# Two V projections of a half visit moved ahead of the scores on TensorE, in the attention of a six-layer network

## What is computed

```python
for i in range(DEPTH):                                  # DEPTH = 6
    x = attn_layer(shift_tokens(x), Wqkv[i], q_scale[i], k_scale[i], Wo[i]) + x
    x = ffn_layer(shift_tokens(x), ln_g[i], ...) + x

def attn_layer(x, Wqkv, qs, ksc, Wo):
    q, k, v = jnp.split(x @ Wqkv, 3, -1)                # 16 heads x 64
    q = l2norm(q) * qs;  k = l2norm(k) * ksc            # then rotary products on q and k
    out = local_attention(q, k, v)                      # windows of 32 queries x 64 keys
    return out.transpose(0, 2, 1, 3).reshape(b, n, INNER) @ Wo
```

## Time and profile before

| | |
|---|---|
| median of 3 runs | 5682.57 us (5681.54 to 5702.88) |
| the profiled execution's own time | 5641.73 us |
| its span in the trace | 5639.9 us |
| TensorE clock granted over the span | 0.916 of full |
| stretch of the six layers | about 1265 to 5600 us |
| busy in the span: PE, PEld, DVE, ACT, POOL | 4558.5, 3064.2, 3371.8, 2396.0, 2573.2 us |

### The profile page before, as it was taken

The page is one execution under the profiler, slowest core; times in us unless marked ns, Lnnn a source line. Parts: engine busy times, 40 slices in busy tenths (PEclk is TensorE's granted clock), DMA queues, the critical chain, the costliest instruction groups (busy, mean ns, idle before and its releaser), DMA issues. The chain is left out here.

```text
span 5639.9 us, 183409 instructions
## 1 busy us (share of the span) xinstructions
PE 4558.5 (81%) x70227; PEld 3064.2 (54%) x70227; DVE 3371.8 (60%) x7024; ACT 2396.0 (42%) x5161; POOL 2573.2 (46%) x4541
## 2 busy tenths in 40 slices
PE   8999838668888878888888888877788887888885
PEld 6777616544555545555555555555555555555553
DVE  3555441666666666665666666666566665666665
ACT  4555443124444344443444444444434444344441
POOL 0000000107666366663566645656546665366661
PEclk9999869879999999999999999989999999999998
DMA  1000003011111010101110111110101011011100
GB/s 34 4 4 3 1 0 98 6 37 28 26 25 29 24 33 22 29 22 30 26 29 22 28 30 26 24 27 22 37 19 29 22 28 37 19 24 27 28 22 31
DMA packets 76047, 143.02 MB, mean 25 GB/s; under 512 B 19655, under 2 KB 57749, under 8 KB 68117
## 3 DMA queue, kind: packets, MB, share of 16 engines
q1 hardware_dynamic: 75284, 131.92, 9.5%
HBM read 35.40 MB, written 4.19 MB: 7 GB/s over the span
## 5 line engine op out<-in xcount | busy, mean ns | idle before, releaser
L2439 DVE TENSOR_TENSOR n_tt<-n_pp,n_rot 128x1024 f32<-128x1024 f32 x768 | 923.4, 1222 | 693.4 <-ACT n_sq L2307 690.5
L1941 POOL TENSOR_TENSOR n_pre<-n_tt 128x512 f32<-128x512 f32 x768 | 969.9, 1274 | 802.8 <-DVE n_tt L2439 802.6
L2057 PE MATMUL n_pp<-n_wqkv,n_xT 128*128 128x512 f32 x1536 | 811.8, 631 | 6.3 <-ACT n_xT L2302 5.6
L2312 ACT COPY n_V<-n_pp 128x512 f32<-128x512 f32 x384 | 224.7, 585 | 1391.1 <-PE n_pp L2065 1391.1
L1976 POOL TENSOR_TENSOR n_pre<-n_pre,n_rn 128x512 f32<-128x512 f32 x768 | 776.6, 1042 | 36.8 <-POOL n_rn L1964 36.8
L2108 PE MATMUL n_pS<-n_qkT 64*32 64x64 f32 (+1 forms) x24576 | 359.4, 233 | 362.9 <-issue 362.9
L2307 ACT ACTIVATE n_sq<-n_pp 128x512 f32<-128x512 f32 x768 | 457.0, 595 | 158.5 <-PE n_pp L2057 152.8
L2108 PEld LDWEIGHTS n_pS<-n_qkT 64*32 64x32 f32 x24576 | 294.5, 110 | 396.2 <-issue 396.2
L2446 DVE TENSOR_REDUCE n_ss<-n_sq 128x8 f32<-128x512 f32 x768 | 504.2, 676 | 0.0
L2065 PE MATMUL n_pp<-n_wqkv,n_xT 128*64 128x512 f32 x1536 | 484.4, 760 | 0.0
L2074 PE MATMUL n_pp<-ident,n_pre 128*128 128x128 f32 x3072 | 420.7, 280 | 72.2 <-POOL n_pre L1976 70.2
(11 more groups left out here) (263 smaller groups left out, 7918.6 us busy)
## 6 DMA issues: line engine op xcount, KB each, us to landing
n_Vx<-n_V SPq DMA_DIRECT2D x192, 256.0 KB, 3.9
n_Vx<-n_V SPq DMA_DIRECT2D x192, 192.0 KB, 3.2
n_wqkv<-in_L_ffn_Wqkv SPq DMA_DIRECT2D x6, 1536.0 KB, 7.4
e_w<-in_L_ffn_w SPq DMA_DIRECT2D x32, 256.0 KB, 3.0
m_Y<-e_ye SPq DMA_DIRECT2D x64, 64.0 KB, 2.0
n_wo<-in_L_ffn_Wo SPq DMA_DIRECT2D x6, 512.0 KB, 7.2
a_xs<-in_L_attn_x SPq DMA_DIRECT2D x16, 128.0 KB, 2.1
x_kept<-X SPq DMA_DIRECT2D x1, 2048.0 KB, 8.6
```

The lines of the kernel that those rows point to most:

```text
L1941: nc.gpsimd.tensor_tensor(d, s[0], s[1][:, :, ::-1, :], ALU.add).then_inc(s_add, 1)
L2057: nc.tensor.matmul(pp[:, c % 2, :], xT[:, j * P:(j + 1) * P], wqkv[:, t * I + 512 * half:t * I + 512 * half + 512], start=True, stop=True) ...
L2439: nc.vector.tensor_tensor(tt[:, c % 4, :, :].rearrange("p s (h d) -> p s h d", d=D), bcast(pp[:, c % 2, :].rearrange("p (h d) -> p h d", d ...
```

## The change

In every half visit that has `nxt`, the two `project_v` calls stand between `weigh` and `scores` instead of behind `scores`. The wait for the turned q and k (`s_qkT`), which stood ahead of the masks, goes with them: it now stands behind `weigh`, ahead of the V projections. In the last visit of a layer all stays as it was. The code of the other engines is the same.

```diff
                     elif prev:
                         weights_ready(pairs[0], N - 1, 1 - u, 1)
-                    after(pe, s_qkT, 8 * N + 4 * j + 4)
+                    if not nxt:
+                        after(pe, s_qkT, 8 * N + 4 * j + 4)
                     masks(N, j)
                     if j == 1:
                         weigh(u, 0)
                     elif prev:
                         weigh(1 - u, 1)
+                    if nxt:
+                        after(pe, s_qkT, 8 * N + 4 * j + 4)
+                        project_v(N + 1, 2 * j, bank("v", 2 * j, 1))
+                        project_v(N + 1, 2 * j + 1, bank("v", 2 * j + 1, 1))
                     scores(j)
                     if nxt:
-                        project_v(N + 1, 2 * j, bank("v", 2 * j, 1))
-                        project_v(N + 1, 2 * j + 1, bank("v", 2 * j + 1, 1))
                         project_qk(N + 1, 4 * j)
                         project_qk(N + 1, 4 * j + 1)
```

## The result

Four runs of the changed kernel have a median of 5491.33 us (5486.06 to 5502.58), against 5688.01 us (5681.54 to 5702.88) for the kernel before on the same chips: ratio 0.9653, 95% interval 0.9626 to 0.9680, 197 us less. The forecast was 5595 us, 87 less than the median that it was taken off; its range, 5480 to 5685, holds the time only just. The direction was right, and nearly every row that was to show a step moved as foretold, but the gain was over twice as large.

What follows compares the result with a forecast made beforehand. It took TensorE's order, with instruction-block stalls in the scores, to bound the kernel. Terms 111 x 0.07 + 39 x 1.55 + 30 x 0.45 + 5 = 87 us, off the median's 5682.6, gave 5595 us; range 5480 to 5685.

Steps and rivals of the forecast that it cites:

- Step 1: Instruction stall in the scores: V ahead of them cuts it from 1.95 to 0.4 us per half visit.
- third rival: The stall stays (chance 0.10): each run of scores pays a fixed stall, wherever V stands; 5866 us.
- the second with its stall of 0.8 us: Rival "even" (chance 0.16): next block comes later, or POOL's last norm holds the turns of q and k; 5668 us.
- Step 2: Behind the scores: V's 1.87 us covered a chain to the second output turn; only 0.42 us come back.
- first rival: All comes through (chance 0.12): no wait opens behind the scores, V's move costs nothing; 343 us less, 5340.
- Step 3: Clock during V projections: of 69 slow half visits, 39 turn fast, gaining 1.55 us each; 30 stay slow, gaining 0.45.
- 39 x 1.55: Term for half visits whose V turns from slow to fast: 39 of them at 1.55 us each, 60 us.
- stays near 92 us: Issue stall ahead of the weighing, 91.6 us in 84 pieces, was to remain unchanged.
- Step 4: Moved wait for turned q and k: worth at most its 5.6 us idle ahead of the masks, taken as 5.
- stall r: Stall left in the scores per half visit: 0.4 us expected, bounds 0 and 1.0, break-even at 0.88.

Runs made afterwards that it cites:

- e5: Changed kernel with the wait back ahead of the masks and the V projections in the middle of the scores: 5620.12 us, ratio 0.9925 to the kernel before.
- e6: Changed kernel with the wait back ahead of the masks and the V projections in the middle of the weighing: 5524.36 us, ratio 0.9762 to the kernel before.
- e4: Changed kernel with add_attention on DVE between the first two rotates instead of behind both: 5304.36 us, ratio 0.9359 to the kernel before.
- e9: Kernel before with add_attention on DVE between the first two rotates, V projections still behind the scores: 5652.44 us, ratio 0.9951.
- e10: e4 with ACT's first square ahead of the first exponential: 5254.44 us, ratio 0.9250 to the kernel before.
- e3: Kernel before with only the wait moved behind the weighing, plus one counter increment, V left behind the scores: 5597.39 us, ratio 0.9877.
- e2: Changed kernel with the wait for turned q and k put back ahead of the masks: 5498.11 us, ratio 0.9715 to the kernel before.
- e1: The kernel before once more, no edit, for a second profiled execution: 5663.93 us, ratio 1.0004.

## Why the prediction was right and wrong

**Step 1, the stall: right.** A block of 256 instructions comes some 3.5 to 4 us after the one before was entered; 0.4 us per half visit were to be left, and 75.7 / 180 = 0.42 are. e5 shows that V has to stand ahead of the stall, and e6 that a place just ahead of the block will do. The third rival, a fixed stall, is out, and the second with its stall of 0.8 us or a new wait for POOL (the turns of q and k wait 56.0 us for its norms, 70.2 before). The Trainium skill, "Runtime: NRT & Kernel Launch", section "Instruction fetch mechanics", calls the cost of a block mostly hidden. In rows of 5.9 ns an instruction it was not: 362.9 us.

**Step 2, what V covered: right.** In the half visit shown, 5.81 us against 5.85, and a wait of 1.61 against 1.65; e4, e9 and e10 show that it is that chain. The first rival is out. For half visits at the full clock the sum of steps 1 and 2, -0.07 us each, came in at -0.09, in part because misses cancel: over the 89, weighing to V takes 0.32 us more, scores 1.72 less (forecast 1.55), and from the end of the scores, V left out, 1.31 more (forecast 1.45).

**Step 3, the clock: the step that failed, by its size.** The mechanism was right, and so was the number of slow half visits left (30 against 29, in the place foretold). The term "39 x 1.55" was too small in both factors. A half visit that turns fast gained 2.61 us, not 1.55. Of the 1.06 us between them, 0.62 are the stall in the weighing, which the forecast held fixed ("stays near 92 us"); 0.20 are a stall in the scores of 2.16 us, where I gave every slow half visit the mean of 1.95; 0.38 are the stretch behind, which already took 4.71 us before in these 56 where I had 4.33 from one of them, so the chain's 5.85 costs less; V gave 0.16 less (1.36 where I had 1.52). Over the 56 that is 59 us. And I had 39 of them, from one mean of 760 ns, where the trace has 56: 17 x 1.55 is 26 us. Together these are the whole way from the 60 us of that term to the measured 146. A mean V is a blunt count: many of before's slow V were only partly at the lower clock.

**Step 4, the moved wait: wrong.** Priced at its own idle time, 5 us; e3 measured 70 us for it alone by the ratio, and with V moved it is 7 to 35 us. It acts on the stall in the weighing: of the fall from 1.57 to 0.62 us in the second half visits of the body, 0.63 us come with the wait (e2 against the changed kernel). So its gain is a part of what step 3 lacked and isn't to be added to it.

**The base.** The sum was taken off an execution 46 us under the median of before, and the median of after lies 4 us over its own profiled execution. 197 - 155 = 42 us of the result are this difference. e1's profile shows more slow V (83 half visits against 77) at the same stalls and is 20 us longer, so about half of it is that the execution that I worked from had fewer slow half visits than usual. Where the rest comes from is open; the medians of before on the other chips were 5660.55, 5667.1 and 5675.08 us, not 5688. Taking the sum off the median as it stood left this out.

That the range holds the time is luck: its lower part was kept for a smaller stall r and for V fast everywhere, and neither came.

## What to carry to other kernels

Where a long run of very short TensorE instructions shows idle time that waits for nothing, count the instructions between two such pauses; if the count is the same each time, put long instructions that are needed anyway within or just ahead of that stretch, and try the semaphore wait ahead of it in another place. Before moving work, ask what it was cover for: here the 1.87 us of V gave back only 0.55 behind the scores (the mean of the 89 half visits at the full clock), until two lines on DVE and one on ACT shortened the chain that it had covered. And price a stall not by its mean but where it stands: two of them in one half visit go with the lower clock.

## What was not expected of the hardware

- A wait that costs next to nothing by its own idle time (5.6 us in all) was worth 70 us where it stood (e3), through stalls of the instruction supply in the weighing behind it (1.57 against 0.65 us in the second half visits of the body).
- Long instructions spared most of the stall also where they stood 40 instructions ahead of a block's border, and not where they stood 102 ahead (e6: means of 0.60 and 2.15 us).
- Executions of one and the same kernel differ in how many V projections run at 1.2 GHz and little else: two profiled ones are 20 us apart (mean 760 and 780 ns) with stalls of 362.9 and 363.8 us.
